# A four-part layer pipeline with routed experts: three changes in the written-out order of the engines' work

## The chip, the cores and the metric

The kernel runs on one core of a Trainium2 chip. The metric is the device time of one launch in microseconds (us). A core has four engines that compute, each with its own instruction stream, carried out strictly in order: TensorE (PE: matrix products and transposes into PSUM), VectorE (DVE), ScalarE (ACT) and GpSimd (POOL). SyncE (SP) only starts DMA transfers. The engines meet at semaphores alone: an instruction that waits holds up everything behind it on its own engine.

## The reference, cut to what matters

Two batches of 2048 tokens, 256 wide, pass through four parts, each behind a layer norm and a modulation:

- **attention**: gated linear attention, 4 heads, in chunks of 64 tokens. Per chunk the scores are a masked product of queries and keys, `A = where(tril, qg @ k_intra.T, 0)`, and the chunk's output is `A @ v` plus the queries times a running state. The output is normed, gated by `silu(g)`, multiplied by `Wo` and added to `x` (this sum is called the attention sum here);
- **a small feed-forward part** (64 channels with 16 inner units);
- **a state-space scan**: 512 channels with 16 states each, `state = state * (1 - dtv * k*k) + (x * dtv) * k` along the tokens, and `y = sum over the 16 states of state * q`, then `D * x` is added, and the result is gated by `silu(z)` and projected;
- **routed experts**: 8 experts, each takes the 512 best tokens of each batch, with GELU between two products.

## The kernel before, in words

The tokens are cut into 16 blocks of 256. The first three parts are a software pipeline over the blocks: in turn `i` the attention of block `i + 2` (stage A), the feed-forward part and the inputs of the scan of block `i + 1` (F), the scan of block `i` (S), the projection of block `i - 1` (C) and the gate scores of block `i - 2` (G) run beside one another. Turns -1 to 17 are written out. Turns 1 to 14 hold A, F and S; turn 15 holds no A, turn 16 no F, and turn 17, with C and G alone, is woven into the experts' code.

A turn has 64 places, `n = 0 ... 63`. Each engine walks the places in order and issues what the table `AT` (line 60) puts at each. Work of a stage that is given a place above 63 runs in the next turn, at that place less 64. There is no planner: this table and the order of the calls in the functions `turn_pe`, `turn_act`, `turn_dve` and `turn_pool` (lines 1452 to 1526) are the order of the instructions. At one place, scan work comes first, then the feed-forward part, the projection, the gate, and attention last.

The scan of a block runs over its 16 states `m`:

- ACT forms the decay rows, two halves per state (`dec_t`, line 1160), at places 6, 8, 10, ...;
- PE transposes them into the banks `pD` (`dec`, line 1130), two halves per state, at every odd place from 11. The half at place `n` waits until the scans of place `n - 2` have read their bank;
- POOL writes the state's input, `inp` (line 1198), at places 14, 18, ... It multiplies `u` by a broadcast row. The first one of a block waits for `u`;
- DVE scans, two instructions per half (line 1179), at every odd place from 13; the half at place `n` needs the transposes of place `n - 2`;
- POOL multiplies the scanned state by its `q` row, `rd` (line 1188), at places 23, 27, ..., into `sq`, which has two buffers: the product of state `m` waits until both halves of the sum of state `m - 2` are done;
- PE adds the product to the block's sum in `pY`, again by transposes (`sum`, line 1147), in two halves of 128 tokens, four transposes each: the first half at places 22, 26, ... and the second two places on, at 24, 28, ... Before the first of them the bank of each half is opened with `D * x` (`open0` at 21, `open1` at 24, line 1138).

`u` (line 1113) is `x * dtv` for the block: two DVE instructions at place 69, that is place 5 of the turn of the block's own scan, behind that place's scans. Its operands are ready since place 61 of the turn before (`ut`, line 892). The PE transposes `turn_b` (line 585, place 8) wait for it too, since they write a bank that it reads.

The other work that the change passes by or that the prediction follows, all on PE unless said: `G0` (line 631, place 27, the first of two running sums of the gates, read by the exponentials of ACT at lines 747 and 748), `turn_c` (line 585, place 35, read by ACT at line 594 into `hB`, which `inx0`, line 926, place 38, multiplies), `inz1` (line 936, place 51, read by ACT at line 1031, behind which ACT writes `dkq`, line 1036, for the transposes `kturn`, line 948, place 53), `dt1` (line 957, place 55, read by ACT's sigmoid at line 1040, behind which ACT forms the denominator, the gate `sg` and the square of the attention's output, line 803), and `wo` (line 722, place 67, that is 3). On DVE, `x_attn` (line 1057, place 4) adds the attention to `x` and takes the statistics of the next norm, and `scored1` (line 845, place 53) is the masked copy of the second pair of heads' scores, which PE computes at place 54 (`sc1`, lines 606 and 611).

Of the kernel before, what the change touches and what calls it, by code (L numbers as in the profile page):

```python
# [23 lines left out]
NT = TB // P  # L24
# [6 lines left out]
DI, DS, DR, DCV = 512, 16, 64, 4  # L31
# [28 lines left out]
AT = dict(  # L60
    stat_a=0, ln_a=2, rows_a=4, turn_a=6, mod_a=7, low=8, v=17, lr=14, v_s=17, z=21, abs=21, exl=23, gk=27, G0=27,
    G1=28, eG0=25, eG1=27, ends=28, q0=31, k0=33, queries0=36, keys0=36, sc0=39, kgt0=38,
    scored0=42, kv0=42, q1=44, queries1=45, states0=51, k1=48, keys1=51, sc1=54, kgt1=54, scored1=53, kv1=55, g=58,
    sg=59, states1=57, S0=27, o=59, o_sq=60, ms=61, o_n=61, rms=65, og=66, wo=67, x_attn=4, ln_b=6, rows_b=6,
    turn_b=8, mod_b=8, win=13, s_f=13, relu0=17, relu1=24, facc0=23, facc1=28, wout=29, x_ffn=30, ln_c=31,
    rows_c=33, turn_c=35, mod_c=34, halo=38, inx0=38, xcp0=38, inx1=43, xcp1=44, tail=45, conv0=43, conv1=47,
    xs0=45, xs1=46, inz0=50, sz0=46, dkq_mm=50, dkq=52, inz1=51, sz1=52, kturn=53, kk=53, dt0=53, dt1=55, sig0=54,
    sig1=56, den=57, nd=60, ut=61, u=69, yz0=19, yz1=19, yt0=21, yT0=20, yt1=22, yT1=22, out=25, x_scan=28, ln_d=40,
    rows_d=42, turn_d=74, mod_d=75, score=79, scores=81, dec=11, sum=22, open0=21, open1=24, dec_t=6, saved=21,
    scan=13, rd=23, inp=14)  # L70


# [318 lines left out]
def layers(nc, block, sem, x_rows, consts, weights, folds, wmod0, wmod1, out_rows, xn_d,  # L391
           scores, fixed, ones_s, ident_s, col1, gb1, W, w_in, xg, select, w_ds):
    with ExitStack() as ctx:
# [89 lines left out]
        def part(at, name):  # L483
            a, n = at[name]
            return room[:, a:a + n]
# [5 lines left out]
        ndT, u = part(room_at, "ndT"), part(room_at, "u")  # L491
# [626 lines left out]
        def nth(n, name, every):  # L1118
            return (n - AT[name]) // every if (n - AT[name]) % every == 0 else -1

        def scan_pe(pe, it, n):
            half = nth(n, "dec", 2)
            if 0 <= half < 2 * DS:
                m, h = half // 2, half % 2
                if h == 0:
                    pe.wait_ge(sem("dec_t"), it * 2 * DS + 2 * m + 2)
                pe.wait_ge(sem("scanned"), it * DT * DS + 2 * half - 2)
                for k2 in range(2):
                    for t in range(NT):
                        i = pe.transpose(pD[h][:, k2 * TB + t * P:k2 * TB + (t + 1) * P],  # L1130
                                         decT[:, m % 2, t, (2 * h + k2) * P:(2 * h + k2 + 1) * P], ident_s[:, :])
                i.then_inc(sem("dec_mm"), 1)
            for t in range(NT):
                if n == AT[f"open{t}"]:
                    pe.wait_ge(sem("xs"), it * 2 + 2)
                    pe.wait_ge(sem("yz"), it * 2 - 1 + t)
                    for k in range(DT):
                        i = pe.matmul(pY[:, t, k * P:(k + 1) * P], xs[:, k, t * P:(t + 1) * P], dskip[:, k, :],
                                      start=(k == 0), stop=False, skip_group_check=True)
                    i.then_inc(sem("opened"), 1)  # L1140
            piece = nth(n, "sum", 2)
            if 0 <= piece < 2 * DS:
                m, t = piece // 2, piece % 2
                if t == 0:
                    pe.wait_ge(sem("read_out"), it * DS + m + 1)
                for k in range(DT):
                    i = pe.matmul(pY[:, t, k * P:(k + 1) * P], sq[:, m % 2, k, t * P:(t + 1) * P], ident_s[:, :],  # L1147
                                  start=False, stop=(m == DS - 1), is_transpose=True, skip_group_check=True)
                i.then_inc(sem("summed"), 1)
# [302 lines left out]
        def turn_pe(pe, i, stages, steps=range(STEPS)):  # L1452
            a, f, s, c, g = blocks_of(i, stages)
            if i == 0:
                pe.wait_ge(sem("weights2_in"), 16)
            if i == 1:
                pe.wait_ge(sem("early"), 1)
            for n in steps:
                if i < 1:
                    early_pe(pe, n + (i + 1) * STEPS)  # L1460
                for it, m in ((c, n + STEPS), (s, n), (f, n - STEPS)):
                    if it is not None:
                        scan_pe(pe, it, m)
                for it, m in ((s, n + STEPS), (f, n)):
                    if it is not None:
                        front_pe(pe, it, m, c)
                if c is not None:
                    back_pe(pe, c, n, f)
                if g is not None:
                    gate_pe(pe, g, n + STEPS, f)  # L1470
                for it, m in ((f, n + STEPS), (a, n)):
                    if it is not None:
                        attn_pe(pe, it, m)
                choose_pe(pe, i, n)
                if i < 1:
                    filler(pe, n + (i + 1) * STEPS)
# [512 lines left out]
```

## Time and profile before

| | us |
|---|---|
| median of 3 runs | 1814.18 (1814.15 to 1815.84) |
| the profiled execution | 1818.58 |
| its span, first to last instruction | 1816.8 |
| PE busy (share of the span) | 1669.8 (92%) |
| DVE busy | 1469.6 (81%) |
| POOL busy | 1370.2 (75%) |
| ACT busy | 1315.2 (72%) |

A line of the timeline gives the start and the length of a run of equal instructions, what they are, and in brackets how long the engine stood idle before them and who released it. Matmuls overlap their neighbours in such a line (four transposes are given with 0.60 us); the chain of waits gives the time by which the work moves on (0.44 us for the same four).

### The profile page before, as it was taken

The numbers are of one execution on the slowest core, as the hardware profiler recorded it, in microseconds if no ns is written. First come the engines' busy times: TensorE is split into PE (matmuls) and PEld (weight loads), VectorE is DVE, ScalarE is ACT, GpSimd is POOL, SyncE is SP. The second block draws the span as 40 slices with busy tenths as digits, with TensorE's granted clock in tenths as the row PEclk, the third lists the DMA queues.
The fourth block names the chain that finished last, engine by engine and source line by source line (L and its number), as shares of the span: only waits on it lengthen the run. The fifth ranks groups of instructions, "written<-read, shape, count | busy, mean of one in ns | idle before, by whom it ended". The sixth has DMA issues, their size and how long they took to land.

```text
span 1816.8 us, 34000 instructions
## 1 busy us (share of the span) xinstructions
PE 1669.8 (92%) x12301; PEld 1439.4 (79%) x12301; DVE 1469.6 (81%) x3084; ACT 1315.2 (72%) x2689; POOL 1370.2 (75%) x644
## 2 busy tenths in 40 slices
PE   6879999999999999999999999997777999999998
PEld 5768787887878888787887878786666888899997
DVE  3648889898988989898898989888987678766663
ACT  3567878888787888879788887876643855666664
POOL 0009899999999999999999999999997343444443
PEclk9999999999999999999999999999987999999999
DMA  5011112212211221221122212212212444455552
GB/s 198 1 59 53 60 65 76 83 53 83 77 60 66 86 73 54 83 76 63 62 87 71 64 72 77 71 62 85 76 63 90 116 132 101 117 140 140 139 136 28
DMA packets 69463, 149.79 MB, mean 82 GB/s; under 512 B 5936, under 2 KB 43312, under 8 KB 68912
## 3 DMA queue, kind: packets, MB, share of 16 engines
q1 hardware_dynamic: 57008, 130.84, 20.9%
q0 software_dynamic: 12288, 16.79, 5.4%
q8 instruction: 98, 1.61, 0.4%
q14 instruction: 69, 0.57, 0.1%
HBM read 121.91 MB, written 17.30 MB: 77 GB/s over the span
## 4 chain that ended last, share of the span: by engine, by line
PE 62%; DVE 13%; ACT 13%; issue 6%; POOL 4%; DMA 0%; DVEq 0%; ACTq 0%; POOLq 0%
PE po L1844 10%; PE ph L1844 9%; PE pD L1130 8%; DVE room L1179 7%; PE pY L1147 7%; PE pA L731 6%; POOL room L1188 3%; PE pB L926 3%; PE pB L936 3%; PE pB L1226 3%; ACT room L1160 2%; PE pA L722 2%; PE pB L957 2%; PE pB L942 2%; PE pA L652 1%
## 5 line engine op out<-in xcount | busy, mean ns | idle before, releaser
L1198 POOL TENSOR_TENSOR room<-room 128x1024 f32<-128x1024 f32 x256 | 609.2, 2380 | 154.0 <-DVE room L1113 133.8
L1179 DVE TENSOR_TENSOR_SCAN room<-pD,last,room 128x256 f32<-128x256 f32 x1024 | 688.7, 730 | 38.7 <-PE pD L1130 25.6
L1188 POOL TENSOR_TENSOR room<-room 128x1024 f32<-128x1024 f32 x256 | 608.6, 2378 | 47.4 <-PE pY L1147 47.3
L1160 ACT ACTIVATE room<-room,kkT 128x512 f32<-128x512 f32 x512 | 359.8, 716 | 57.7 <-PE pD L1130 56.4
L1130 PE MATMUL pD<-fixed,room 128*128 128x128 f32 x2048 | 320.6, 280 | 67.0 <-DVE room L1179 57.5
L1147 PE MATMUL pY<-fixed,room 128*128 128x128 f32 x2048 | 319.5, 280 | 14.8 <-POOL room L1188 14.8
L1130 PEld LDWEIGHTS pD<-fixed,room 128*128 128x128 f32 x2048 | 242.0, 144 | 98.9 <-issue 50.1
L1147 PEld LDWEIGHTS pY<-fixed,room 128*128 128x128 f32 x2048 | 249.2, 145 | 67.0 <-POOL room L1188 30.9
L343 POOL DMA_INDIRECT xg<-xn_rows,W x64 | 67.6, 1056 | 196.7 <-DVE W L337 181.4
L1803 ACT ACTIVATE h<-ph 128x512 f32<-128x512 f32 x128 | 76.7, 599 | 137.6 <-PE ph L1844 137.6
L1844 PE MATMUL po<-w_up,h_up 128*128 128x256 f32 x512 | 149.5, 292 | 3.2 <-DVE h_rest L1711 2.6
L1711 DVE TENSOR_TENSOR h_rest<-h,h_up 128x512 fp32r<-128x512 f32 x128 | 85.0, 689 | 76.0 <-ACT h_up L1770 75.5
L1844 PE MATMUL po<-w_up,h_rest 128*128 128x256 f32 x512 | 145.3, 284 | 0.0
L1844 PE MATMUL po<-w_rest,h_up 128*128 128x256 f32 x512 | 145.0, 283 | 0.0
L1900 POOL DMA_INDIRECT y_out<-ys,W x64 | 110.1, 1720 | 42.2 <-DVE ys L1752 25.2
L731 PE MATMUL pA<-hA,W 128*128 128x256 f32 x512 | 121.0, 380 | 1.6 <-DVE w_in L817 1.6
L731 PEld LDWEIGHTS pA<-hA,W 128*128 128x128 f32 x512 | 92.6, 190 | 12.5 <-DVE w_in L817 2.4
L1844 PEld LDWEIGHTS po<-w_up,h_up 128*128 128x128 f32 x512 | 98.3, 192 | 4.9 <-DVE h_rest L1711 4.0
L1844 PE MATMUL ph<-hg_up,w_up 128*128 128x512 f32 x256 | 102.1, 399 | 0.0
L1844 PE MATMUL ph<-hg_rest,w_up 128*128 128x512 f32 x256 | 101.0, 395 | 0.0
L1844 PE MATMUL ph<-hg_up,w_rest 128*128 128x512 f32 x256 | 101.0, 395 | 0.0
L1844 PEld LDWEIGHTS po<-w_up,h_rest 128*128 128x128 f32 x512 | 98.5, 192 | 0.0
(315 smaller groups left out, 3418.0 us busy)
## 6 DMA issues: line engine op xcount, KB each, us to landing
room<-kq_rows SPq DMA_DIRECT2D x128, 512.0 KB, 3.7
w_in<-w_d SPq DMA_DIRECT2D x32, 1024.0 KB, 5.7
room<-ndS SPq DMA_DIRECT2D x16, 512.0 KB, 3.2
xt<-x_in SPq DMA_DIRECT2D x16, 256.0 KB, 2.9
y_out<-xo SPq DMA_DIRECT2D x16, 256.0 KB, 2.1
xn_rows<-xnC SPq DMA_DIRECT2D x16, 256.0 KB, 2.2
W<-weights SPq DMA_DIRECT2D x1, 1808.0 KB, 9.2
W<-weights SPq DMA_DIRECT2D x1, 1697.5 KB, 16.8
```

Source lines behind the costliest of these rows:

```text
L343: pool.indirect_dma_start(xg[:, k % 2, s, :], None, xn_d[0:(k // E + 1) * T, :], bass.IndirectOffsetOnAxis(ap=self.ids[:, k * SL + s:k * S ...
L731: i = pe.matmul(bank[:, h2 * TB:(h2 + 1) * TB], wt[:, c, h * DK:(h + 1) * DK], hA[:, c, :], start=(c == 0), stop=(c == DC - 1))
L1130: i = pe.transpose(pD[h][:, k2 * TB + t * P:k2 * TB + (t + 1) * P], decT[:, m % 2, t, (2 * h + k2) * P:(2 * h + k2 + 1) * P], ident_s[:, :])
L1147: i = pe.matmul(pY[:, t, k * P:(k + 1) * P], sq[:, m % 2, k, t * P:(t + 1) * P], ident_s[:, :], start=False, stop=(m == DS - 1), is_transp ...
L1160: act.activation(decT[:, m % 2, t, :], turn2(ndT, it, NT * DI, t * DI, DI), ACT.Copy, bias=1.0, scale=turn2(kkT, it, NT * DS, t * DS + m, ...
L1179: dve.tensor_tensor_scan(run, pD[h][:, k2 * TB:(k2 + 1) * TB], run, last[:, bass.ds(later(it) * (DS * DT) + m * DT + k, 1)], ALU.mult, ALU ...
L1188: pool.tensor_tensor(sq[:, m % 2], st[:, m % 4], kqb[:, m % SLOTS, 1, :].unsqueeze(1).broadcast_to([P, DT, TB]), ALU.mult).then_inc(sem("r ...
L1198: pool.tensor_tensor(st[:, m % 4], turn2(u, it, DT * TB).rearrange("p (k t) -> p k t", k=DT), kqb[:, m % SLOTS, 0, :].unsqueeze(1).broadca ...
L1711: dve.tensor_tensor(rest, whole, upper.bitcast(F32), ALU.subtract).then_inc(sem(done), 1)
L1803: act.activation(h1[:, f % 4, :], ph[:, f % 2, :], ACT.Gelu).then_inc(sem("gelu"), 1)
L1844: m = pe.matmul(to, stationary(c, p0), moving(c, p1), start=(c == 0 and n == 0), stop=(c == chunks - 1 and n == 2))
L1900: pool.indirect_dma_start(out_rows, bass.IndirectOffsetOnAxis(ap=select.ids[:, k * SL + s:k * SL + s + 1], axis=0), ys[:, k % 2, s, :], No ...
```

## The change

Three edits, all to the order of instructions; every instruction of before is issued after, with the same operands.

- `sum`: the second half of a state's sum stands one place behind the first, at 23, 27, ..., and no longer two. At that place it comes behind the decay transposes and ahead of whatever the other stages have there. `open1` moves with it, from place 24 to 23.
- `u`: from place 69 to 68. At place 4 it comes ahead of `x_attn`, and so ahead of the scans of place 5.
- `scored1`: from place 53 to 55, where it comes behind that place's pair of scans.

```diff
     stat_a=0, ln_a=2, rows_a=4, turn_a=6, mod_a=7, low=8, v=17, lr=14, v_s=17, z=21, abs=21, exl=23, gk=27, G0=27,
     G1=28, eG0=25, eG1=27, ends=28, q0=31, k0=33, queries0=36, keys0=36, sc0=39, kgt0=38,
-    scored0=42, kv0=42, q1=44, queries1=45, states0=51, k1=48, keys1=51, sc1=54, kgt1=54, scored1=53, kv1=55, g=58,
+    scored0=42, kv0=42, q1=44, queries1=45, states0=51, k1=48, keys1=51, sc1=54, kgt1=54, scored1=55, kv1=55, g=58,
     sg=59, states1=57, S0=27, o=59, o_sq=60, ms=61, o_n=61, rms=65, og=66, wo=67, x_attn=4, ln_b=6, rows_b=6,
     turn_b=8, mod_b=8, win=13, s_f=13, relu0=17, relu1=24, facc0=23, facc1=28, wout=29, x_ffn=30, ln_c=31,
     rows_c=33, turn_c=35, mod_c=34, halo=38, inx0=38, xcp0=38, inx1=43, xcp1=44, tail=45, conv0=43, conv1=47,
     xs0=45, xs1=46, inz0=50, sz0=46, dkq_mm=50, dkq=52, inz1=51, sz1=52, kturn=53, kk=53, dt0=53, dt1=55, sig0=54,
-    sig1=56, den=57, nd=60, ut=61, u=69, yz0=19, yz1=19, yt0=21, yT0=20, yt1=22, yT1=22, out=25, x_scan=28, ln_d=40,
-    rows_d=42, turn_d=74, mod_d=75, score=79, scores=81, dec=11, sum=22, open0=21, open1=24, dec_t=6, saved=21,
+    sig1=56, den=57, nd=60, ut=61, u=68, yz0=19, yz1=19, yt0=21, yT0=20, yt1=22, yT1=22, out=25, x_scan=28, ln_d=40,
+    rows_d=42, turn_d=74, mod_d=75, score=79, scores=81, dec=11, sum=22, open0=21, open1=23, dec_t=6, saved=21,
     scan=13, rd=23, inp=14)
 
 
@@ -1138,9 +1138,10 @@
                         i = pe.matmul(pY[:, t, k * P:(k + 1) * P], xs[:, k, t * P:(t + 1) * P], dskip[:, k, :],
                                       start=(k == 0), stop=False, skip_group_check=True)
                     i.then_inc(sem("opened"), 1)
-            piece = nth(n, "sum", 2)
-            if 0 <= piece < 2 * DS:
-                m, t = piece // 2, piece % 2
+            for t in range(NT):
+                m = nth(n - t, "sum", 4)
+                if not 0 <= m < DS:
+                    continue
                 if t == 0:
                     pe.wait_ge(sem("read_out"), it * DS + m + 1)
                 for k in range(DT):
```

## Rows read from the trace of the kernel before

**Rows 1.** The page's first part: busy time, share of the span, instructions.

```profile
PE 1669.8 (92%) x12301; PEld 1439.4 (79%) x12301; DVE 1469.6 (81%) x3084; ACT 1315.2 (72%) x2689; POOL 1370.2 (75%) x644
```

**Rows 2.** Busy time by stretch (columns named in the first line): turns 10 and 15.

```profile
core 0: us, PE busy (x) PEld busy (x) DVE busy (x) ACT busy (x) POOL busy (x), PEclk, DMA share, GB/s
781.10:860.20 79.10, 75.08 (x583) 64.16 (x582) 70.55 (x141) 65.75 (x140) 74.58 (x33) 1.00 0.21 71
...
1237.90:1314.50 76.60, 59.72 (x384) 49.92 (x383) 69.66 (x177) 48.86 (x105) 74.28 (x32) 0.93 0.21 70
```

**Rows 3.** Waits of POOL, 781.1 to 860.2 us: total, times, longest.

```profile
POOL room L1188 <- PE pY L1147: 3.2, 3, 1.7
POOL room L1198 <- PE pY L1147: 1.0, 1, 1.0
```

**Rows 4.** Waits of PE in the same stretch.

```profile
PE pD L1130 <- DVE room L1179: 2.7, 2, 1.6
...
PE pY L1147 <- POOL room L1188: 0.3, 1, 0.3
```

**Rows 5.** Timeline of POOL: start, length, line, shapes, idle before and releaser.

```profile
824.57 2.36 POOL L1188 TENSOR_TENSOR room<-room 128x1024 f32<-128x1024 f32 x1 [1.70 <-PE pY L1147]
...
842.82 2.37 POOL L1198 TENSOR_TENSOR room<-room 128x1024 f32<-128x1024 f32 x1 [0.96 <-PE pY L1147]
...
854.47 2.35 POOL L1188 TENSOR_TENSOR room<-room 128x1024 f32<-128x1024 f32 x1
...
1237.85 2.36 POOL L1198 TENSOR_TENSOR room<-room 128x1024 f32<-128x1024 f32 x1 [0.86 <-PE pY L1147]
```

**Rows 6.** The chain of waits, 785 to 847 us: start, time, what.

```profile
785.46 0.91 PE pA L631 x8
...
790.03 0.66 PE pD L1130 x4
...
797.64 1.86 PE pB L926 x8
...
818.83 0.28 PE pB L948 x2
...
820.16 0.44 PE pY L1147 x4
...
822.24 0.87 PE pB L957 x2
...
836.39 1.87 PE pA L722 x8
...
841.48 1.18 DVE room L1113 x2
...
846.58 0.66 PE pD L1130 x4
```

**Rows 7.** Timeline of ACT at the four products that it waits for.

```profile
786.39 0.60 ACT L747 ACTIVATE w_in<-pA 128x512 f32<-128x512 f32 x1 [1.78 <-PE pA L631]
...
796.43 1.02 ACT L594 ACTIVATE hB<-pB,col 128x256 f32<-128x256 f32 x2 [1.74 <-PE pB L585]
...
817.72 0.60 ACT L1031 ACTIVATE szT<-pB 128x512 f32<-128x512 f32 x1 [1.35 <-PE pB L936]
...
823.13 0.58 ACT L1040 ACTIVATE pB<-pB 128x512 f32<-128x512 f32 x1 [0.74 <-PE pB L957]
```

**Rows 8.** Timeline of DVE at the masked copy, the gated output and the attention sum.

```profile
821.77 0.45 DVE L845 COPY_PREDICATED att<-causal,pA 128x256 f32<-128x256 uint8 x1 [1.79 <-PE pA L611]
...
831.33 0.69 DVE L879 TENSOR_TENSOR w_in<-pA,sg 128x512 f32<-128x512 f32 x1 [0.30 <-ACT w_in L803]
...
836.12 1.38 DVE L1179 TENSOR_TENSOR_SCAN room<-pD,last,room 128x256 f32<-128x256 f32 x2
838.28 0.69 DVE L1057 TENSOR_TENSOR xt<-xt,pA 128x512 f32<-128x512 f32 x1 [0.79 <-PE pA L722]
```

**Rows 9.** Timeline of PE in turn 15, behind its longest wait.

```profile
1268.04 1.11 PE L1130 MATMUL pD<-fixed,room 128*128 128x128 f32 x4 [3.23 <-DVE room L1179]
```

## The prediction

> **What bounds the kernel now.** The first part of the page says that PE is busy for 92% of the span and the other engines for 72 to 81% [rows 1]. Busy shares over the whole span mix the pipeline with the experts, so the second view is the busy time by stretch. One turn in the middle of the pipeline takes 79.1 us; POOL works 74.58 us of it and PE 75.08 us [rows 2]. Two engines are nearly full, and each has about 4 us of gaps. Either could be the bound, and the change touches the gaps of both.
>
> The waits tell them apart only in part. POOL waits 3.2 us a turn for the halves of a state's sum before `rd`, and 1.0 us before an `inp` [rows 3]. PE waits 2.7 us for DVE's scans and 0.3 us for POOL [rows 4]. The reader is to see next where POOL's gaps lie: the longest, 1.70 us, ends at 824.57, and the last at 842.82 [rows 5]. That last one stands before the first `inp` of a block, which waits for `u`; the chain has `u` running from 841.48 for 1.18 us, to 842.66 [rows 6]. The releaser printed there is PE, but PE's second half of that place had long been done. So POOL, with all its gaps before, still came 0.96 us too early for `u`: the gaps at 818 to 830 us cost nothing by themselves.
>
> The chain of waits then shows who is late. It runs on PE, and leaves PE for ACT or DVE at five places a turn, each time because PE must wait for an answer to something that it has itself just computed. Those five places decide the case [rows 6 to 8]:
>
> 1. `G0` (785.46, 0.91 us) releases ACT, which had waited 1.78 us; behind its exponentials ACT forms the decay rows for which PE waits until 790.03.
> 2. `turn_c` releases ACT at 796.43, after 1.74 us; `inx0` on PE starts at 797.64, as ACT's 1.02 us are over.
> 3. `inz1` releases ACT at 817.72, after 1.35 us; behind it comes `dkq`, for which `kturn` waits until 818.83.
> 4. `dt1` (822.24, 0.87 us) releases ACT at 823.13, after 0.74 us. ACT then has no gap until the squares at line 803, DVE waits 0.30 us for those at 831.33, and behind DVE's work there the decay transposes of place 3 wait.
> 5. `wo` (836.39, 1.87 us) releases `x_attn` on DVE at 838.28, after 0.79 us; behind it come the norm's statistics and the scans for which the transposes of place 7 wait.
>
> POOL appears in the chain once, at 854.47: from `u` it runs five operations without a gap, then the first `rd` of the block, and PE waits 0.3 us for that.
>
> **The second half of the sum.** Nothing is added: 32 groups of four transposes a turn stay, and one takes 0.44 us on PE (820.16) [rows 6]. What changes is what stands behind them. At the places 27, 35, 51, 55 and 3 the group now comes directly ahead of `G0`, `turn_c`, `inz1`, `dt1` and `wo`; before, it came one place later, behind them. Places 31, 39, 43, 59 and 15 are like them, but what is late there (`q0`, `sc0`, `inx1`, the output `o`, `score`) is read by nobody who waits: the chain does not leave PE there. Everything on PE from the next place on has its old time. So each of the five starts is 0.44 us later, and since the reader behind each had been waiting for it (1.78, 1.74, 1.35, 0.74 and 0.79 us), the answer is 0.44 us later too, and PE, which had no slack on it, waits that much longer. That is 5 x 0.44 = 2.2 us a turn. It can't be below nothing: in an engine that works in order, moving a group ahead brings nothing else forward. Two of the five could have a little cover (at `turn_c` I find 0.2 us at most between ACT's end, 797.45, and 797.64), and a group behind a wait takes 0.66 us (846.58) [rows 6], so a turn's bounds are 1.8 and 3.3 us; I take 2.2, by the group without a wait.
>
> What it is there to shorten, POOL's wait for sums, it does shorten: the half at 824 comes 1.7 us sooner, since `dt1` (0.87 us) and the 0.9 us of products behind it no longer stand before it. But POOL gains only an earlier arrival at the first `inp`.
>
> **`u` ahead of the attention sum.** The scans of place 3 start at 836.12 and take 1.38 us; `x_attn` starts at 838.28, after 0.79 us of waiting for `wo` [rows 8]. `u` takes 1.18 us [rows 6]. Alone it would make `x_attn` 0.4 us late. With `wo` 0.44 us later the gap is 0.79 + 0.44 = 1.23 us, so it just fits, and `x_attn` is late by `wo` alone, which is counted. No DMA and no queue but DVE's is passed. What it returns is at the scans of place 7 and on, which stood behind `u`: the chain ran through `u` and three pairs of scans to 846.58, where PE had waited 0.28 us and its group took 0.66 in place of 0.44. That 0.50 us goes; next late is the norm's result for `turn_b` and the first products of attention, 2.2 us later than before, so no more can be had. The first `inp` follows `u`: with four of the delays in, `u` ends at 836.12 + 1.3 + 1.76 + 1.18 = 840.4, POOL gets there at about its old 842.8, and its `rd` of 854.47 is done when PE, 1.7 us late, comes. PE's 0.3 us of wait goes with its 0.22 us of slow start, 0.52 us. Return: 0.50 + 0.52 = 1.0 us a turn, with bounds of 0.5 (one of the two) and 1.3 us (`u` itself and the 0.1 behind it).
>
> **The masked copy.** It waits 1.79 us for scores, with the scans of place 55 behind it [rows 8]. With the pair first, DVE fills 1.3 us of this wait. But what DVE has behind it ends in the wait of 0.30 us for ACT at 831.33, and that ACT work is late by edit one. So it is worth nothing: DVE waits there 0.3 us and more instead. Behind the copy, PE's `g` at place 58 needs it, and it still comes three places sooner. If the cover went, the worth would be at most the 1.3 us a turn.
>
> **The sum.** A turn: 2.2 - 1.0 = +1.2 us, 80.3 in place of 79.1. Turns 1 to 14 have this shape; the first `inp` of turn 15 stands at 1237.85, five turns behind 842.82, so 79.0 each [rows 5]. 14 x 2.2 = 30.8 us of delay, 13 x 1.0 = 13.3 (at 1.02) returned at the turns' seams, and at the last seam, into turn 15, 1.2 us, since from there on it is DVE and POOL that are followed and `u` gives them the whole 1.18. Turn 15 has PE at 59.72 of 76.60 us [rows 2]: no cost there. 30.8 - 13.3 - 1.2 = +16.3 us. Against the profiled execution's 1818.58 that is 1835; that execution is 4.4 us above the median of the runs, so the runs should show 1814.2 + 16.3, about 1831.
>
> The most-contended engine is POOL or PE by busy time. The Trainium skill (Perfetto Trace Analysis, Identifying the Most-Contended Engine and Optimization Strategy) says to take occupancy for GpSimd but weight-load time for TensorE, and then to close the gaps of the engine found. Weight loads fill 64.16 us of the turn [rows 2], so by this rule POOL is the bound, and closing its gaps is a gain; this speaks against my forecast, and its result is the first rival. The chain of the same turn disagrees with it.
>
> **Rivals.** *POOL is the bound, and its gaps close.* For it: 74.58 of 79.1 us, and 4.2 us of waits a turn that the edits address [rows 2, 3]. Against it: POOL waits for `u` behind all of them. PE's 75.08 us would be next, so 4.0 us a turn go at most: 14 x 4.0 = 56, and 1758 us. Chance 0.10. *The delays are covered and `u` pays:* PE has work that I take as bound to the five answers but that isn't, so edit one costs nothing, and 14 x 1.0 = 14 us are gained: 1800. It decides from the point where fewer than about 2.3 of the five delays (1.0 / 0.44) reach the chain. Chance 0.10. *Half and half:* two of the five reach it, 14 x (0.88 - 1.0) and so 1812, or three, 1818. Chance 0.13. *Nothing comes back:* the 0.5 us at the transposes of place 13 and at the first sum are taken by the later `x_attn`; all 30.8 us stay: 1845. Chance 0.13. *PE's clock falls.* In turn 15 a wait of 3.23 us, behind another, is followed by four transposes of 1.11 us in place of 0.63 [rows 9], while the steady turns have a granted clock of 1.00 [rows 2]. PE's gaps grow by 1.2 us a turn, but their longest stays near 1.6 us. If the clock did fall once a turn for four groups, at 0.48 us each, 14 x 2 = 28 us more come on top: 1859. Chance 0.04.
>
> The Trainium skill (TensorE: Matmul & The Clock Gate, Part 1) has the clock drop to half after idle time and come back under load. The trace agrees in turn 15 and shows no drop in the steady turns; by that rule, if the new waits counted as idle enough, the last rival's 1859 holds, and otherwise 1831.
>
> The forecast has 0.50, with its own range of 1820 to 1840. The range for 8 in 10 goes from 1798, so that `u` alone is in, to 1848, with all delays and no return (1845), or the upper bound of 3.3 us a turn with it (14 x 2.3 = 32, 1846). A measurement of this kernel tells about 0.2%, 3.6 us, from no change. Slower has the forecast's 0.50, 0.17 of the cases without return and with the lower clock, and 0.06 of the half; same has the other 0.07 of the half; faster has the first two rivals: 0.73, 0.07 and 0.20.
>
> **What would show it.** Right: turns of about 80.3 us; POOL's waits before `rd` at 824 and 830 shorter, and its gap before the first `inp` gone; PE's waits at the transposes of place 31 and at `kturn` at 0.8 in place of 0.4 and 0.3 us; DVE waiting 0.8 us or more for line 803; no wait of PE for POOL at the first sum. Wrong: PE's waits at these two unchanged, or the chain on POOL through the turn.

## The result and the profile after

| | us |
|---|---|
| before, median of 4 runs | 1815.01 (1814.15 to 1821.28) |
| after, median of 4 runs | 1841.07 (1840.23 to 1842.51) |
| ratio after / before | 1.0138, 95% interval 1.0126 to 1.0151 |
| profiled execution after; its span | 1841.85; 1840.1 |

The change makes the kernel 26 us slower; 16 were forecast. 1841.07 is 1 us above the forecast's own range (1820 to 1840) and inside the range for 8 in 10 (1798 to 1848). The busy time by stretch shows two neighbouring turns (the columns as in [rows 2]):

```profile
756.60:836.90 80.30, 74.67 (x581) 64.16 (x582) 71.03 (x139) 65.72 (x140) 74.49 (x33) 1.00 0.20 70
836.90:918.60 81.70, 76.15 (x582) 65.32 (x582) 70.93 (x139) 65.90 (x140) 74.67 (x33) 0.98 0.20 69
```

A turn takes 80.3 us, or 81.7, where it took 79.1 [rows 2]. PE and POOL do the same work, so both have larger gaps. The second turn has a lower clock and 1.5 us more of busy time on PE.

The waits of PE from 756.6 to 836.9 us (who waited for whom: total, times, longest), to be read against [rows 4]:

```profile
PE pD L1130 <- DVE room L1180: 3.0, 2, 1.9
PE pD L1130 <- ACT room L1161: 0.8, 1, 0.8
PE pB L948 <- ACT dkq L1036: 0.8, 1, 0.8
PE pA L714 <- ACT w_in L803: 0.5, 1, 0.5
PE pB L926 <- ACT hB L594: 0.3, 1, 0.3
```

The waits for ACT at place 31 (line 1130) and at `kturn` (line 948), 0.39 and 0.33 us before, have grown by 0.44 us each. Two waits of PE for ACT are new in this list: 0.5 us at line 714, which comes behind `dt1`, and 0.3 us at `inx0` (line 926), which comes behind `turn_c`. The wait for DVE has grown by 0.3, and the one for POOL is gone. DVE waits 0.9 us for the squares of line 803, where it waited 0.3. The timeline of ACT has the same four products as [rows 7]:

```profile
803.63 0.60 ACT L747 ACTIVATE w_in<-pA 128x512 f32<-128x512 f32 x1 [1.85 <-PE pA L631]
814.10 1.02 ACT L594 ACTIVATE hB<-pB,col 128x256 f32<-128x256 f32 x2 [2.73 <-PE pB L585]
...
835.82 0.60 ACT L1031 ACTIVATE szT<-pB 128x512 f32<-128x512 f32 x1 [1.79 <-PE pB L936]
841.67 0.58 ACT L1040 ACTIVATE pB<-pB 128x512 f32<-128x512 f32 x1 [1.18 <-PE pB L957]
```

At `inz1` and `dt1` it waits 0.44 us longer than before (1.35 and 0.74 us), which is one group of the sum; at `turn_c` it waits 1.0 us longer, and at `G0` 0.07, since its work before `G0` has become later too.

POOL's timeline, against [rows 5], shows what the sooner sums were worth to it:

```profile
752.62 2.36 POOL L1199 TENSOR_TENSOR room<-room 128x1024 f32<-128x1024 f32 x1 [2.10 <-issue]
760.58 2.36 POOL L1189 TENSOR_TENSOR room<-room 128x1024 f32<-128x1024 f32 x1 [0.96 <-PE pY L1148]
766.18 2.37 POOL L1189 TENSOR_TENSOR room<-room 128x1024 f32<-128x1024 f32 x1 [0.94 <-DVE room L1180]
769.75 2.37 POOL L1199 TENSOR_TENSOR room<-room 128x1024 f32<-128x1024 f32 x1 [1.20 <-ACT last L1166]
```

The wait of 1.70 us for a sum is down to 0.96, and the one before the first `inp` is gone. The one at 830, which was to shrink too, is still 0.94 us, now with DVE as its releaser. Others have come: POOL waits 5.8 us a turn now, where it waited 4.2 by [rows 3]. 1.2 us are for ACT and 0.9 for DVE; for 2.7 us the profile shows no releaser.

A measure for what follows is the start of `kturn` (line 948) in one turn to that in the next. Rows of after, from PE's timeline:

```profile
756.58 0.28 PE L948 MATMUL pB<-fixed,dkq 32*128 32x32 f32 x2 [0.77 <-ACT dkq L1036]
...
836.93 0.28 PE L948 MATMUL pB<-fixed,dkq 32*128 32x32 f32 x2 [0.77 <-ACT dkq L1036]
...
918.60 0.28 PE L948 MATMUL pB<-fixed,dkq 32*128 32x32 f32 x2 [0.77 <-ACT dkq L1036]
```

This gives 80.35 and 81.67 us. Before, a turn was 79.02 us by it, and none of the middle ones above 79.4.

### The profile page after: what moved, and what is told of

The parts are those of the page before. It is cut to its first block, busy times and chain, and to the rows that moved or that the text cites. A ratio compares the mean times of both kernels' runs of the same rounds, so it can differ in the third digit from the quotient of the medians.

```text
span 1840.1 us, 34000 instructions
## 1 busy us (share of the span) xinstructions
PE 1671.8 (91%) x12301; PEld 1445.7 (79%) x12301; DVE 1476.0 (80%) x3084; ACT 1316.5 (72%) x2689; POOL 1369.8 (74%) x644
## 4 chain that ended last, share of the span: by engine, by line
PE 65%; ACT 15%; DVE 11%; issue 5%; POOL 2%; DMA 0%; DVEq 0%; ACTq 0%; SPq 0%; POOLq 0%
PE po L1845 9%; PE ph L1845 9%; PE pD L1130 8%; PE pY L1148 8%; PE pA L731 6%; DVE room L1180 5%; PE pB L926 3%; PE pB L936 3%; PE pB L1227 3%; ACT room L1161 2%; PE pB L957 2%; PE pB L942 2%; POOL room L1189 2%; PE pY L1138 1%; PE pA L652 1%
## 5 line engine op out<-in xcount | busy, mean ns | idle before, releaser
L1148 PE MATMUL pY<-fixed,room 128*128 128x128 f32 x2048 | 312.8, 279 | 9.2 <-POOL room L1189 9.2
```

## The experiments

Each ratio is to runs of the kernel before on the same chip. The turn is the usual one among those with a granted clock of 1.00 from start to end; longer ones with the lower clock are named beside it.

| kernel | median us | ratio (95% interval) | turn us |
|---|---|---|---|
| after | 1841.07 | 1.0138 (1.0126 to 1.0151) | 80.35; six of 81.5 to 81.9 |
| 1 halves of the sum only | 1852.56 | 1.0201 (1.0182 to 1.0220) | 81.08; seven of 81.5 to 81.9 |
| 2 `u` only | 1813.63 | 0.9986 (0.9975 to 0.9996) | 78.74; one of 80.07 |
| 3 copy only | 1816.00 | 1.0001 (0.9990 to 1.0012) | 79.03 |
| 4 five halves put back | 1808.95 | 0.9953 (0.9938 to 0.9968) | 78.60; two of 79.7 to 80.0 |
| 5 after, with PE kept at work | 1835.17 | 1.0097 (1.0076 to 1.0119) | 80.35 |
| 6 only the five moved | 1844.76 | 1.0148 (1.0128 to 1.0168) | 80.35; five of 81.5 to 82.0 |
| 7 four first halves behind | 1807.66 | 0.9939 (0.9923 to 0.9956) | 77.55; eight of 78.7 to 78.8 |
| 8 less work for POOL | 1808.24 | 0.9953 (0.9936 to 0.9970) | 78.80 |
| 9 four halves put back | 1809.23 | 0.9947 (0.9929 to 0.9964) | 78.59; two of 79.7 to 80.0 |
| 10 as 7, with PE kept at work | 1794.00 | 0.9871 (0.9852 to 0.9889) | 77.54 |
| 11 as 10, copy at place 53 | 1801.02 | 0.9894 (0.9874 to 0.9915) | 77.54 |

**1, 2 and 3: each part alone.** Against the changed kernel, the first has (parts of two lines of the table)

```diff
-sig1=56, den=57, nd=60, ut=61, u=68,
+sig1=56, den=57, nd=60, ut=61, u=69,
-sc1=54, kgt1=54, scored1=55, kv1=55, g=58,
+sc1=54, kgt1=54, scored1=53, kv1=55, g=58,
```

and the other two have, in the kernel before, only `u=68` or only `scored1=55`.

> Only the halves of the sum are moved (and the opening with them); u and the masked copy stay where they were. Theory (five starts on PE are 0.44 us late, each with a reader that waits): 14 x 2.2 = 31 us and no return, 1845 us, up to 1855 if PE's clock falls in some turns; PE's wait at the first sum of a block stays. Rival (POOL's waits for sums are the bound): faster than before, 1770 to 1805. Rival (the whole loss comes from u or the copy): 1814.

> Only u is one place sooner. Theory: x_attn is 0.4 us late, since wo is not, and 0.5 us come back at the transposes of place 13 and 0.5 at the first sum of a block: 0.6 us a turn, 1806 us (1802 to 1811). Rival (a later attention sum is paid in full and nothing returns): 1814 + 14 x 0.4 = 1820. Rival (POOL, which waits 0.96 us a turn for u, is the bound): 1814 - 14 = 1800.

> Only the masked copy of the second scores is behind the pair of scans. Theory: DVE fills its 1.79 us of waiting, but waits that much longer for ACT's squares: 1814, within 2 us. Rival (DVE is late in this stretch): up to 1.3 us a turn, 1796.

The sum's halves alone cost 81.08 - 79.02 = 2.06 us a turn, and 37 us in all, with the lower clock in eight turns: the rival in which POOL gains by sooner sums is gone. `u` alone gives 0.28 us a turn, half of what was expected, and its median of 1813.6 us lies above the expected 1802 to 1811. The copy gives nothing. From the first kernel to the changed one, which adds both, it is 81.08 - 80.35 = 0.73 us a turn: that is `u`'s return when the attention sum is late anyway.

Where the 2.06 us arise can be read on PE, from the start of `kturn` to that of the transposes of place 7, in the kernel before and then in kernel 1:

```profile
818.83 0.28 PE L948 MATMUL pB<-fixed,dkq 32*128 32x32 f32 x2 [0.33 <-ACT dkq L1036]
...
841.62 0.63 PE L1130 MATMUL pD<-fixed,room 128*128 128x128 f32 x4 [1.63 <-DVE room L1179]
```

```profile
1000.99 0.28 PE L948 MATMUL pB<-fixed,dkq 32*128 32x32 f32 x2 [0.77 <-ACT dkq L1036]
...
1024.53 0.63 PE L1130 MATMUL pD<-fixed,room 128*128 128x128 f32 x4 [1.94 <-DVE room L1180]
```

The stretch is 22.79 us and then 23.54, 0.75 longer, and 0.44 of that is already there at the transposes of place 3, behind `dt1`. So `wo` adds 0.31. Behind place 31, `inx0` and the next `kturn` the delay is 1.18, 1.62 and 2.06 us, 0.44 more each time, for `G0`, `turn_c` and `inz1`.

**4 and 6: which halves.** The fourth kernel puts back the five, the sixth moves these five alone (there the tuple holds the eleven other places).

```diff
             for t in range(NT):
                 m = nth(n - t, "sum", 4)
-                if not 0 <= m < DS:
+                late = (27, 35, 51, 55, 67)
+                if t == 1 and n % 4 == 0:
+                    m = nth(n - 2, "sum", 4)
+                if not 0 <= m < DS or t == 1 and (n % 4 == 0) != (AT["sum"] + 4 * m + 1 in late):
                     continue
```

> The change as it is, but at places 27, 35, 51, 55 and 3 the second half of the sum stands where it stood before, behind the products G0, turn_c, inz1, dt1 and wo; the eleven other halves stay moved. Theory: all of the loss goes and the return of u stays, 1806 us (1802 to 1811), turns of 78.5 us. Rival (the other eleven cost too, or the loss is not in these five): 1820 to 1841. Rival (POOL gains by sooner sums): below 1800.

> The change, but of the sixteen second halves only the five at places 27, 35, 51, 55 and 3 are moved; the eleven others stand where they stood before. u and the copy are moved. Theory: all of the loss is in these five: turns of 80.35 us and 1841 us, within 5 us for the turns with the lower clock. Rival (the halves at the other places carry part of it): 1815 to 1835.

Moving only the five gives the changed kernel's 80.35 us to the hundredth, and putting them back gives 78.60: all of the steady loss is in these five, and the other eleven cost nothing. (Kernel 4 is 0.14 us a turn below kernel 2, from which it differs by the copy and these eleven; by PE's starts the gain arises at places 31 to 33, and its cause stays open.) PE's waits at place 31 and at `kturn` are at their old size in the fourth kernel:

```profile
787.39 0.66 PE L1130 MATMUL pD<-fixed,room 128*128 128x128 f32 x4 [0.39 <-ACT room L1164]
...
816.18 0.28 PE L948 MATMUL pB<-fixed,dkq 32*128 32x32 f32 x2 [0.33 <-ACT dkq L1036]
```

**9: four of the five.** As 4, with `late = (27, 35, 51, 55)`.

> The change, with four of the five second halves put back (27, 35, 51, 55); the one ahead of wo stays moved, to place 3. Theory: u and the half ahead of wo cost x_attn the same 0.4 us, and one hides the other, so this one is free once u is moved: turns of 78.6 us as with all five back, 1809 us. Rival (each half costs its 0.44 us): turns of 79.0 us, 1815.

78.59 against 78.60 us: with `u` moved, the half ahead of `wo` is free. And 80.35 - 78.59 = 1.76 us is 4 x 0.44: the other four cost a whole group each. The chain of waits of the changed kernel shows why (start, time, what):

```profile
774.31 1.38 DVE room L1180 x2
775.69 1.18 DVE room L1113 x2
776.87 0.62 DVE xt L1057
```

`x_attn` follows `u` at once, and no longer `wo`. The two delays lie beside one another.

**5: the turns of 81.7 us.** The kernel is the changed one with eight more transposes at the end of place 6, whose result nobody reads:

```diff
+                if n == 6 and c is not None and f is not None:
+                    for _ in range(8):
+                        pe.transpose(pA[1][:, 2 * P:3 * P], ident_s[:, :], ident_s[:, :])
```

The timeline of PE in the changed kernel has this place in a turn of 80.35 us, and then in one of 81.67:

```profile
780.13 0.63 PE L1130 MATMUL pD<-fixed,room 128*128 128x128 f32 x4 [1.95 <-DVE room L1180]
...
782.00 0.62 PE L645 MATMUL pA<-hA,W 128*16 128x128 f32 x8 [0.28 <-ACT hA L594]
782.54 0.66 PE L1130 MATMUL pD<-fixed,room 128*128 128x128 f32 x4
```

```profile
860.47 0.63 PE L1130 MATMUL pD<-fixed,room 128*128 128x128 f32 x4 [1.95 <-DVE room L1180]
...
862.34 1.04 PE L645 MATMUL pA<-hA,W 128*16 128x128 f32 x8 [0.15 <-ACT hA L594]
863.31 1.12 PE L1130 MATMUL pD<-fixed,room 128*128 128x128 f32 x4
```

The four transposes take 1.12 in place of 0.66 us, and the busy time by stretch has the clock (third number from the right) at 0.50, the lower of its two levels:

```profile
860.00:862.00 2.00, 1.53 (x12) 1.28 (x12) 2.00 (x4) 1.91 (x5) 2.00 (x2) 0.95 0.63 240
862.00:864.00 2.00, 1.85 (x12) 1.21 (x12) 0.89 (x2) 1.80 (x5) 2.00 (x1) 0.50 0.06 23
```

> The changed kernel with eight transposes of 0.11 us each, written to an unused part of a bank, at the end of place 6, inside PE's wait of 1.95 us for DVE; they add to no result. Theory (in 7 of 14 turns PE's clock halves behind this wait and the turn is 1.3 us longer): the wait falls to about 1.1 us, no turn has the lower clock, all take 80.35 us, and 9 us come back: 1832 us. Rival (the longer turns have another cause): 1841, or 1848 if the fillers' 0.9 us are not covered.

Of the thirteen turns with the long wait none is longer than 80.7 us now, the clock is 1.00 in all of them, and the ratio falls from 1.0138 to 1.0097. The median, 1835, is 3 us above the expected one. The transposes fill part of the wait, and 1.07 us of it are left:

```profile
771.69 1.04 PE L1480 MATMUL pA<-fixed 128*128 128x128 f32 x8
773.80 0.63 PE L1130 MATMUL pD<-fixed,room 128*128 128x128 f32 x4 [1.07 <-DVE room L1180]
```

So it is PE's idle time that brings the lower clock. Turn by turn against kernel 5, it costs 1.1 to 1.3 us in each of seven turns: the six long ones, and turn 2 with 80.65 in place of 79.45 us. From the first `kturn` to the last it is 1204.56 - 1195.85 = 8.7 us. Over the kernels: where this wait is 1.6 us (before, 3, 8) or 1.1 (5, 10, 11), none of these thirteen turns has the lower clock; where it is 1.9 us (after, 1, 2, 4, 6, 7, 9) some have, from one (2) to nine (7).

**8: is POOL the bound?** In the kernel before, POOL's product leaves out one of the four channel groups, so that this kernel does not compute the function (`[...]` stands for the rest of an index):

```diff
-pool.tensor_tensor(sq[:, m % 2], st[:, m % 4], kqb[...].unsqueeze(1).broadcast_to([P, DT, TB]),
+pool.tensor_tensor(sq[:, m % 2, 0:3], st[:, m % 4, 0:3], kqb[...].unsqueeze(1).broadcast_to([P, 3, TB]),
```

> The kernel before, with POOL's product rd over three of the four channel groups only (the fourth is left out, its old content is summed): 16 x 0.6 = 9.5 us less work a turn for POOL. Theory: POOL is no bound, and only PE's 0.3 us of wait at the first sum and the 0.2 us of slow start behind it go: 0.5 us a turn, 1807 us. Rival (POOL's 74.6 of 79.0 us are what holds the turn): 4 us a turn, down to PE's 75, 1760 us.

POOL does 66.09 us of work a turn in place of 74.6, and the turn is 0.22 us shorter:

```profile
737.80:816.60 78.80, 75.08 (x582) 64.16 (x583) 70.57 (x140) 65.68 (x140) 66.09 (x33) 1.00 0.21 71
```

Of 8.5 us taken off an engine that was 94% busy, 97% went into its waits. The median, 1808, is as expected (1807), but the turn gives less than the expected 0.5 us. From the first to the last `kturn` the kernel is 4.4 us shorter: 1.1 in turn 2, 0.6 in turn 15 and about 0.22 in each of the twelve between. What is left of the gain lies outside them.

**7, 10 and 11: the same in the other direction.** If a product that another engine waits for should come first, then the first halves that stand ahead of four of them should go behind as well. On top of the fourth kernel:

```diff
+                if t == 0 and n + 1 in (27, 35, 51, 55):
+                    continue
...
+                if s is not None and n in (27, 35, 51, 55):
+                    first_half(pe, s, (n - 1 - AT["sum"]) // 4)
```

The second part stands at the end of a place in `turn_pe`; `first_half` waits for `read_out` and issues the same four transposes. Kernel 10 has the eight idle transposes too, and 11 is 10 with `scored1=53`.

> As with the five halves put back, and besides the first halves that stand at places 26, 34, 50 and 54 are issued behind G0, turn_c, inz1 and dt1, at the end of places 27, 35, 51 and 55. Theory (a product that is waited for should be the first thing that PE does): G0 brings the 0.39 us of PE's wait behind it, turn_c 0.15, inz1 0.33 and dt1 0.44, 1.3 us a turn: turns of 77.3 us, 1791 us. Rival (PE's own work or POOL is the bound as soon as a wait closes): 1809, as with the five put back, or above it since POOL gets these sums later.

> The four first halves behind their products, five second halves where they were, u and copy moved, and the eight transposes that keep PE at work at place 6. Theory: that kernel's 77.55 us turns were 78.7 where PE's clock was halved, in ten of them; now all are 77.55: 1814.2 - 14 x 1.45 = 1794 us. Rival (the fillers' 0.9 us are paid where DVE is late anyway): 1805 or more.

> The same with the masked copy back at place 53, ahead of the pair of scans. Theory: ACT now begins its long stretch behind dt1 sooner, DVE has less cover, and the copy's wait of 1.8 us is partly paid: 0.3 to 0.8 us a turn more than with the copy at 55, 1798 to 1806 us. Rival (DVE still waits for ACT's squares): no difference.

The turn is 77.55 us, 1.05 less than in kernel 4 (1.3 expected). But nine turns have the lower clock, and kernel 7 misses its expected 1791 us by 17; with PE kept at work (10) the usual turn is 77.54 and none has the lower clock, and the median is 1794.0, 1.3% less than before. PE has no wait left at place 31 and at `kturn`; the busy time of kernel 10, and the two waits of PE for DVE that it still has:

```profile
738.20:815.70 77.50, 75.16 (x591) 64.94 (x590) 70.56 (x140) 65.87 (x140) 74.41 (x33) 1.00 0.21 73
```

```profile
824.00 0.63 PE L1137 MATMUL pD<-fixed,room 128*128 128x128 f32 x4 [0.90 <-DVE room L1192]
830.17 0.63 PE L1137 MATMUL pD<-fixed,room 128*128 128x128 f32 x4 [1.06 <-DVE room L1192]
```

The copy at 53 leaves the turn at 77.54 us: the rival was right. DVE waits 0.29 us for ACT's squares with it and 0.94 with the copy at 55, so the copy only moves DVE's wait. The medians of 10 and 11 differ by 7 us, with intervals that overlap. The clock goes with it: the four runs of 11 at 1801 to 1802 us have a mean granted clock of 0.977, its two at 1794.5 and 1795.1 and all of kernel 10 have 0.984 or 0.985. In the two profiled executions (3.7 us apart) 1.3 us lie before the first `kturn`, 1.0 in the turn behind it, where kernel 11 has the lower clock at 156 us and kernel 10 has not, and 1.2 behind the last `kturn`. Why the clock falls there in some runs only stays open.

## Why the prediction was right, and where it was short

- **PE's order is the path, POOL's gaps are not: right.** Shown by 1 (POOL's sums sooner, 37 us slower) and 8 (POOL's work less by 8.5 us, the turn by 0.2). Two of the three waits of POOL that were predicted to shrink did, the third, at 830, stayed at 0.94 us, and others came elsewhere.
- **Five starts, 0.44 us each: right in place, a little high in size.** 2.06 us a turn measured for 2.2. Kernels 4 and 6 show that it is these five and no other. The missing 0.14 us is not at `turn_c`, where the prediction looked for cover: the four without `wo` cost 1.76 us, 4 x 0.44 (9 against the changed kernel), and `wo` adds 0.31 (1).
- **The attention sum: right.** `u` and the delay of `wo` hide one another; 9 shows it, and without the delay (2) `u` brings 0.28 us in place of 0.73.
- **What `u` returns: 0.73 us a turn for 1.0.** By PE's starts from kernel 1 to the changed one, 0.34 us come back at the transposes of place 13 for 0.50 forecast, and 0.38 at the first sum for 0.52. The waits of 0.28 and 0.3 us went. The terms that were too large are the two slow starts of 0.22 us behind them, read from the 0.66 us that the chain gives a group. From the start of a group to that of the next instruction it is 0.49 us at place 13 before (846.58 to 847.07) and 0.44 after, so 0.05 was to be had there. At the first sum it is 0.49 us before, behind the wait, and 0.49 after, without one: nothing was to be had.
- **The copy is worth nothing: right** (3, 11).
- **The clock: the step that failed.** It was put as a rival with 0.04, on the ground that PE's longest wait stays near 1.6 us. That ground was false by the prediction's own terms: `x_attn` and what it releases are 0.44 us later, but PE's work between the transposes of places 3 and 7 is only in another order and ends when it did, so its wait there must grow by about 0.4. It is 1.95 us, 0.3 more. Kernel 5 shows what that cost: the clock fell in seven turns, 8.7 us together. The rival had priced a fall at 2 us, in every turn; one costs 1.1 to 1.3 us.

By the starts of `kturn`, turn 0 to turn 15 take 1177.80 us before, 1195.85 in kernel 5 and 1204.56 in the changed kernel. So of the 26.75 us, 18.05 are there without the lower clock, and 8.7 come with it. The forecast's 16.3 stands against the 18.05. Part of this closeness is luck: a turn was put at 2.2 - 1.0 = 1.2 us and measured at 2.06 - 0.73 = 1.33, and both terms were too large, so that their errors partly cancel.

The rule of the Trainium skill (Perfetto Trace Analysis, Identifying the Most-Contended Engine) named POOL; the runs decide against it here (8: 8.5 us less work, 0.22 us a turn). The rule of the Trainium skill that idle time lowers TensorE's clock (TensorE: Matmul & The Clock Gate, Part 1) agrees with the trace, which has it at 0.50 behind the wait of 1.95 us. What sets the seven turns in which it fell apart from the six others with the same wait, no run here shows.

## What to carry to other kernels

Where two engines are nearly full, look for the instructions whose reader is already waiting when they end, and count what stands directly ahead of them: a group of 0.44 us there cost 0.44 us a round in four of five cases here (0.31 in the fifth), while the same group one place further on was free. Closing a wait on a nearly full engine is worth nothing if that engine waits again, later in the round, for someone on the path. And a change that lengthens a wait of TensorE by a few tenths can pay a second time by its clock; idle transposes inside the wait are a cheap way to find out.

## What the runs showed of the hardware that was not expected

- A wait of TensorE of 1.9 us brings the lower clock in some rounds of a kernel and not in others with the same wait: in seven of thirteen in the changed kernel, in one of thirteen in kernel 2. A fall costs 1.1 to 1.3 us.
- Eight idle transposes (1.04 us in the timeline) inside that wait kept the clock at 1.00 in all thirteen (kernel 5).
- The length that the chain gives a group is not what it costs. The four transposes of the first sum have 0.66 us there before, behind a wait, and 0.59 after, without one; from their start to that of the next instruction it is 0.49 us both times.
